# dt products over all 128 rows of the projection tile instead of 13, in a Mamba-and-experts layer on one core

## The reference, cut to what matters

```
proj = u @ x_proj_w[d]                        # u: tokens x 384, proj: tokens x 44
dt   = softplus(proj[:, :12] @ dt_w[d] + dt_b[d])   # tokens x 384
Bm, Cm = proj[:, 12:28], proj[:, 28:44]
h    = exp(dt * A) * h + (dt * u) * Bm        # scan over the tokens
y    = sum over the states of h * Cm  + u * D_skip
```

## Time and profile before

| | us |
|---|---|
| median of 3 runs | 948.13 (942.41 to 949.29) |
| the profiled execution | 947.83 |
| its span, first to last instruction | 946.1 |
| TensorE matmuls busy | 803.7 (85%) |
| VectorE busy | 734.3 (78%) |
| ScalarE busy | 645.5 (68%) |
| GpSimd busy | 535.2 (57%) |
| mean granted clock of TensorE | 0.912 |

### The profile page before, as it was taken

One profiled execution on the slowest core, in us unless ns is written; L12 is line 12 of the kernel. 1 busy time (PEld: TensorE's weight loads), 2 busy tenths in 40 slices (PEclk: granted clock), 3 DMA queues, 4 the chain that ended last, 5 costly groups with the idle time before them and its releaser, 6 DMA issues.

```text
span 946.1 us, 16644 instructions
## 1 busy us (share of the span) xinstructions
PE 803.7 (85%) x6060; PEld 716.0 (76%) x6061; DVE 734.3 (78%) x873; ACT 645.5 (68%) x1258; POOL 535.2 (57%) x343
## 2 busy tenths in 40 slices
PE   0489795889998999989999899996865699999990
PEld 0223232889998999989999899995764599999990
DVE  3777489779999999999999999997548555555554
ACT  0364576999999999999999999982222344444431
POOL 7420000589997899979999789891000344444420
PEclk9989655899999999999999999997775699999996
DMA  4011101346465664755746567475062111111106
GB/s 84 2 67 60 14 3 45 107 109 182 130 163 168 184 178 133 164 169 150 190 125 160 167 160 196 119 174 192 18 190 85 30 45 46 43 42 42 43 29 208
DMA packets 46453, 104.43 MB, mean 110 GB/s; under 512 B 16448, under 2 KB 25176, under 8 KB 46392
## 3 DMA queue, kind: packets, MB, share of 16 engines
q1 hardware_dynamic: 35784, 74.67, 24.4%
q0 software_dynamic: 8352, 27.07, 14.4%
q10 hardware_dynamic: 2256, 1.87, 0.6%
HBM read 83.77 MB, written 19.82 MB: 109 GB/s over the span
## 4 chain that ended last, share of the span: by engine, by line
PE 51%; DVE 18%; ACT 17%; POOL 7%; issue 4%; DMA 2%; another core or an unknown queue 0%; ACTq 0%; DVEq 0%; POOLq 0%; SPq 0%
PE ps L1409 15%; PE ps L1681 8%; DVE arena L839 8%; PE ps L1518 7%; ACT arena L1255 6%; PE ps L1664 6%; POOL arena L620 5%; ACT arena L1238 4%; PE ps L1669 4%; PE ps L1477 3%; PE ps L1588 3%; PE ps L1429 2%; ACT arena L1241 2%; PE ps L1459 2%; PE ps L1432 1%
## 5 line engine op out<-in xcount | busy, mean ns | idle before, releaser
L620 POOL TENSOR_TENSOR arena<-arena 128x1024 f32<-128x1024 f32 x192 | 395.4, 2286 | 145.3 <-DVE arena L839 142.0
L839 DVE TENSOR_TENSOR_SCAN arena<-arena,ps 128x1024 f32<-128x1024 f32 x192 | 426.5, 2277 | 27.1 <-PE ps L1518 24.6
L1409 PE MATMUL ps<-ident,arena 128*128 128x128 f32 (+3 forms) x2622 | 348.3, 280 | 84.0 <-ACT arena L1122 35.2
L1409 PEld LDWEIGHTS ps<-ident,arena 128*128 128x128 f32 (+3 forms) x2622 | 300.0, 144 | 104.2 <-issue 50.8
L1255 ACT ACTIVATE arena<-arena,neg_a 128x510 f32<-128x510 f32 x384 | 241.2, 711 | 0.0
L624 POOL DMA_INDIRECT arena<-x_rows,arena x39 | 37.7, 968 | 177.4 <-DVE arena L1018 96.5
L1518 PE MATMUL ps<-arena 128*128 128x128 f32 x768 | 102.9, 278 | 0.0
L1518 PE MATMUL ps<-arena,ln_in 128*128 128x128 f32 x768 | 102.3, 277 | 0.0
L1518 PEld LDWEIGHTS ps<-arena 128*128 128x128 f32 x768 | 94.6, 194 | 0.0
L1518 PEld LDWEIGHTS ps<-arena,ln_in 128*128 128x128 f32 x768 | 94.2, 193 | 0.0
L1681 PE MATMUL ps<-arena,ln_in 128*128 x468 | 82.7, 327 | 0.8 <-DVE arena L1049 0.8
(11 more groups left out here) (216 smaller groups left out, 904.8 us busy)
## 6 DMA issues: line engine op xcount, KB each, us to landing
arena<-b_rows SPq DMA_DIRECT2D x64, 512.0 KB, 4.0
arena<-ws SPq DMA_DIRECT2D x16, 576.0 KB, 6.0
arena<-wf POOLq DMA_DIRECT2D x16, 576.0 KB, 7.7
arena<-hf POOLq DMA_DIRECT2D x16, 576.0 KB, 7.5
summed_first<-arena SPq DMA_DIRECT2D x8, 576.0 KB, 5.4
summed_second<-arena SPq DMA_DIRECT2D x8, 576.0 KB, 7.3
arena<-summed_second SPq DMA_DIRECT2D x8, 576.0 KB, 5.7
gates_dram<-arena SPq DMA_DIRECT2D x4, 768.0 KB, 3.5
```

The source lines that it names most:

```text
L620: g_.tensor_tensor(state[i % STATES], state[i % STATES], c_bc[u % C_BUFS], ALU.mult).then_inc(s_mul, 1)
L839: v.tensor_tensor_scan(o, a, x, 0.0, ALU.mult, ALU.add).then_inc(s_scan, 1)
L1409: return mm(o, src, ident[at:at + parts, at:at + parts], start=start, stop=True, is_transpose=True, skip_group_check=True)
```

## The change

The weights of dt get a block for each direction, 128 partitions high. It is cleared to zero, and the 13 rows of the direction are loaded where they were. The product then takes all 128 rows of `lb`: the rows of the other direction, of B and of C meet zeros. VectorE clears the new tile among the setup instructions. Since the tile is 384 words wider, all tiles cut after it move by 1,536 bytes in each partition.

```diff
-        dt_w_sb = cut([DI], parts=64)
+        dt_w_sb = cut([2, DI])
...
-                     (dt_w_sb[0:RANK, :], dt_w[0]), (dt_w_sb[32:32 + RANK, :], dt_w[1]),
+                     (dt_w_sb[0:RANK, 0, :], dt_w[0]), (dt_w_sb[32:32 + RANK, 1, :], dt_w[1]),
...
-                    loads.append((dt_w_sb[32 * d + RANK:32 * d + RANK + 1, P * blk:P * blk + P],
+                    loads.append((dt_w_sb[32 * d + RANK:32 * d + RANK + 1, d, P * blk:P * blk + P],
...
             v.memset(w_x, 0.0)
+            v.memset(dt_w_sb, 0.0)
...
-                        mm(ps[:, DT_BANK + DB * d + blk, :], dt_w_sb[32 * d:32 * d + RANK + 1, P * blk:P * blk + P],
-                           lb[g % 2][32 * d:32 * d + RANK + 1, :], start=True, stop=True).then_inc(s_dt_ps, 1)
+                        mm(ps[:, DT_BANK + DB * d + blk, :], dt_w_sb[:, d, P * blk:P * blk + P],
+                           lb[g % 2], start=True, stop=True).then_inc(s_dt_ps, 1)
```

## The result

The changed kernel takes 938.96 us, median of 9 runs (935.02 to 941.04). The kernel before, run beside it, takes 944.57 us, median of 9 (941.84 to 949.66). The ratio, that of the means (938.79 and 945.54), is 0.9929, 95% interval 0.9901 to 0.9956, so 4 to 9 us less: clear of noise, and inside 1%. The profiled execution took 941.04 us, its span 939.3.

What follows compares the result with a forecast made beforehand. TensorE at half clock in the softplus stage was taken to make VectorE wait; 0.4 + (5.8 - 1.1) = 5.1 us of gain, so 948.1 - 5.1 = 943.0 us, range 938.0 to 948.5.

Steps and rivals of the forecast that it cites:

- The clock follows the rows, and rows of zero weights count: Softplus stage: 128-row dt products hold TensorE's clock up, from 0.59 to 0.8 or more, despite zero weights.
- Rival A: Softplus stage: clock doesn't follow, zero rows don't count, only overlap is lost; 948.9 us, at most 952; chance 0.12.
- The price of a product doesn't depend on its rows: dt products: price goes by columns and clock; three matmuls stream 2.6 us at full clock, 5.2 at half.
- VectorE is the next bound: Softplus stage at full clock: VectorE itself is late next, its waits inside the stage under 1.6 us.
- The sum of 5.1 us: Softplus stage gain: 0.4 us at the first correction plus 5.8 us of VectorE's waits less 1.1 that stay.
- rival B: Softplus stage: TensorE pauses, the clock falls again, half the 5.1 us is lost; 945.6 us; chance 0.18.
- the slack: Softplus rounds at full clock: TensorE and ScalarE finish 2.7 us or more before VectorE needs them.
- the last step: After the stage: the scan stage shifts whole by the gain, and the sum holds for the median, giving 943.0 us.
- The lost overlap: dt products of two directions and transposes no longer side by side: hidden; in rival A 0.8 us, up to 3.7.
- The memset: Setup on VectorE: at most 0.8 us, delaying parameter loads, covered by some 10 us; nothing shows.
- the moved tiles: Tiles cut after the wider weight tile move by 1,536 bytes: zero cost; the range carries 0.5 us either way.
- Rival C: Clock full from the stage's start: first matmuls 2.6, waits 5.8, transposes 1.4, all 9.8 us; 938.3 us; chance 0.10.

Runs made afterwards that it cites:

- e1: Changed kernel with its memset, wider tile and moved tiles, but dt products over 13 rows again: 948.38 us, ratio 1.0003 to the kernel before.
- e2: Changed kernel with dt products over rows 0 to 44 (45 rows): 948.33 us, ratio 1.0006 to the kernel before.
- e3: Changed kernel with dt products over rows 0 to 63 (64 rows): 947.17 us, ratio 0.9996 to the kernel before.
- e5: Changed kernel with dt products over rows 0 to 95 (96 rows): 940.83 us, ratio 0.9928 to the kernel before.
- e7: e4 plus unread filler products ahead of the last dt round and ahead of and behind the last 12 transposes: 937.81 us, ratio 0.9910 to the kernel before.
- e4: Changed kernel plus three unread 128-row filler products ahead of the first dt product: 938.75 us, ratio 0.9911 to the kernel before.
- e6: Kernel before (13 rows) plus three unread 128-row filler products ahead of the first dt product: 942.03 us, ratio 0.9954 to the kernel before.

## Where the prediction was right, and what failed

**The clock follows the rows, and rows of zero weights count.** Right. 0.59 became 0.86. e1 shows that the product's rows alone do it, e2 and e3 that more rows than 13 don't suffice as such, e5 that 96 do. Rival A falls; its argument that zero weights may not count is answered by the changed kernel itself. That the rows must also carry data isn't excluded (e5).

**The price of a product doesn't depend on its rows.** Right: six records take 2.84 us at full clock and 5.49 at half with 128 rows, and the same with 45.

**VectorE is the next bound.** Right: with the clock up it doesn't wait from round 2 to round 6, and its work is unchanged.

**The sum of 5.1 us.** The second L809 was to end at 159 to 160 and ends at 159.33, 5.1 us earlier. That the sum met this so closely is luck, as its terms were less exact. The first group was to bring 0.4 us and brought none: the clock came up 6.2 us after the first product, not 4.0 to 5.2, and so behind the first three matmuls. Round 1 was to keep 1.1 us of waiting and kept 0.36. The waits left are 1.67 us against 1.1, and 0.44 us came from the input stage, where the start of the first product varies from 97.0 to 99.0 among runs with the same code there.

Not in the sum was the fall of the clock ahead of round 7, the mechanism of rival B, which cost 1.31 us. I had put one such fall inside the slack, and had given an odd round 5.0 us at full clock, by the same terms 7.9 at half. I had left out that ScalarE's copy of the transposed B rows, and so all three Abs, stand behind the products and the transposes. Measured, the path is 9.2 us at half clock, against some 7.9 of VectorE's work: the wait. At full clock it would be 2.65 less, 6.6, so the slack of an odd round is about 1.3 us by this estimate and not 2.7.

**What failed is the last step, from the sum to what is measured.** The prediction held that about 1% is what a measurement of this kernel tells from no change, so that a gain of 5.1 us would hardly be seen. Nine runs of each tell it well: the interval, 0.9901 to 0.9956, is 0.3% to either side. And it carried the stage's gain unchanged to the end ("the scan stage shifts as a whole") and to the median ("its sum holds for the median"): 943.0, where 938.96 was measured. The change is 6.7 us by the ratio and 6.8 by the two spans, 1.7 of them behind the stage, a term that the prediction put at nothing. 1.4 of these are one fall of the clock fewer in the scans, and a fall costs some 3 us in the output product (e1). So the rest of the kernel doesn't simply shift: its clock moves single executions by as much as the change is worth.

As a change, 5.1 us (ratio 0.9946) lies inside the measured interval, towards its upper end. The three runs weren't at fault for the level. 948.13 is near the medians of the 29 and 11 later runs of the kernel before, 947.66 and 947.55; the nine beside the changed kernel have 944.57 because five of them are of the faster heap, against 6 of 29 and 4 of 11. Against those later medians the changed kernel is 8.6 to 8.7 us faster, but they weren't taken side by side. Its profiled execution (941.04) is the slowest of its nine, 2.1 us over their median, and what went faster in the others no trace shows. So how much beyond 5.1 us belongs to the edit stays open.

**The lost overlap.** Its price at half clock was mis-sized: 1.9 us in e2, not 0.8. Rival A would have come out at about 950. At full clock it is hidden, as forecast: the transposes at 118.87 stand behind the products and VectorE doesn't wait for what follows them.

**The memset** and **the moved tiles** cost nothing that shows, as forecast (e1).

**Rival C**, 9.8 us, needed filler: e7 has all three of its parts (2.65 at the start, the waits down to 0.9, 1.35 at the transposes) and its stage and ramp are 10.0 us shorter than before. To the first copy of y only 8.7 are left (195.1 and 186.4 us from the first product), so the last part would not have come whole.

## What to carry to other kernels

Read the granted clock beside TensorE's busy share. Where TensorE is busy and the clock is at half, look at how many rows its products span. Rows of zero weights cost no time here and brought the clock from half to full; that is worth something if TensorE is what the others wait for and no overlap of row groups is lost that matters. Pauses of TensorE ahead of a short chain can be filled with products whose result nobody reads. Follow the gain beyond the next instruction: half of what e7 gained at the first scan was lost again in the scans.

When summing a path, go through everything that stands in order on each engine. A copy of 0.28 us, which stood behind the transposes and ahead of the three Abs, was left out here, and with it the wait of 1.31 us.

An effect of half a per cent can't be forecast in absolute time from one traced execution; state the change, and look first at how the runs are spread and at where the clock falls in stages that the change doesn't touch.

## What the runs showed of the hardware

TensorE's clock stays at 1.2 GHz through products of 13 rows that keep it busy (0.50 at 6.10 of 6.10 us) and through the first 12 records of 45 and of 64 rows (0.50 at 10.40 of 10.40 and at 10.50 of 10.50 us). Over the stage it is mostly down with 64 rows (0.63) and mostly up with 96 and 128 (0.83 and 0.86), where the added weights are zero and part of the data is not. Where it falls isn't fixed by the program: at the same instructions it fell in one execution and not in another (e4 and e7, and the output product in before and e1). Two products on rows 0 to 12 and 32 to 44 run side by side: 12 records in 4.18 us at full clock (e6), where 12 records of 128 rows take 5.42 (e4). The Trainium skill, "TensorE: Matmul & The Clock Gate", Part 1, ties the clock to how busy TensorE is; by these runs that alone doesn't do, as the narrow products left it at 0.50 with TensorE busy all the time and the 128-row ones kept it at 1.00 with TensorE busy for 25.85 of 37.30 us.
